# Linear attention of four images: from a loop of single stages to one staggered program

## The reference

```python
t = t + _L2_attn_ref(_ln_t(t), w_qkv, w_out, b_out)      # t: 4 x 1024 x 128, then _ln_t(t) feeds the mixtures

q, k, v = split(x @ w_qkv)                 # 8 heads of 32
k, v = inst_norm(k), inst_norm(v)          # (x - mean) / sqrt(var + 1e-5) over the 32 of a head
dots = einsum('bhnd,bhne->bhde', k, v)
out = einsum('bhnd,bhde->bhne', q, dots) * (1.0 / n)
return out.reshape(b, n, 256) @ w_out + b_out
```

## Time and profile before

| | |
|---|---|
| Median of 3 runs | 2886.87 us (2886.83 to 2897.33) |
| The profiled execution | 2889.75 us |
| Its span, first to last instruction | 2888.0 us |
| Mean granted TensorE clock | 0.781 of full speed |
| PE busy | 1869.1 us (65%) |
| DVE busy | 1648.0 us (57%) |
| ACT busy | 966.2 us (33%) |
| POOL busy | 658.1 us (23%) |

### The profile page before, as it was taken

How to read it: one execution, slowest core, us unless ns; L and a number is a source line. 1 busy time by engine, 2 the same in 40 slices (tenths; PEclk the granted TensorE clock), 3 DMA queues, 4 the chain that set the end, 5 groups by cost and what they waited for, 6 DMA issues and landing times. The chain is left out here.

```text
span 2888.0 us, 25863 instructions
## 1 busy us (share of the span) xinstructions
PE 1869.1 (65%) x8280; PEld 825.4 (29%) x8280; DVE 1648.0 (57%) x3684; ACT 966.2 (33%) x1542; POOL 658.1 (23%) x675
## 2 busy tenths in 40 slices
PE   1564893785686666599658888787886410190089
PEld 1121321321221334456312223232222210090034
DVE  3485776767768654466545756656562121088823
ACT  1232141142132131255326675665664210000133
POOL 2200600420330300044312132332123157500000
PEclk7686896787888776699859999998897655555589
DMA  3301201201200000020021110110000021100030
GB/s 86 80 18 28 59 2 43 58 0 39 50 15 18 7 0 0 0 86 18 14 66 35 27 56 14 30 42 25 24 5 9 5 63 10 8 8 31 2 124 22
DMA packets 58242, 88.62 MB, mean 31 GB/s; under 512 B 17992, under 2 KB 29250, under 8 KB 57866
## 3 DMA queue, kind: packets, MB, share of 16 engines
q1 hardware_dynamic: 47604, 77.66, 9.0%
q10 hardware_dynamic: 6426, 7.99, 1.3%
q0 software_dynamic: 4096, 1.58, 0.8%
HBM read 58.59 MB, written 24.74 MB: 29 GB/s over the span
## 5 line engine op out<-in xcount | busy, mean ns | idle before, releaser
L2150 DVE TENSOR_REDUCE f_half_max<-f_ring 128x1 f32<-128x512 f32 x512 | 334.8, 684 | 306.3 <-PE f_ring L1825 304.1
L2033 ACT ACTIVATE f_probs<-f_ST 128x512 f32<-128x512 f32 x512 | 293.0, 597 | 212.4 <-PE f_ST L1849 208.2
L1825 PE MATMUL f_ring<-f_stacks 96*128 96x512 bf16 x512 | 212.7, 417 | 54.4 <-DVE f_half_max L2150 27.6
L772 DVE TENSOR_REDUCE att_half_max<-att_ring 128x1 f32<-128x512 f32 x256 | 161.1, 683 | 101.4 <-PE att_ring L659 92.7
L1849 PE MATMUL f_ST<-f_stacks 99*128 99x512 bf16 x512 | 203.8, 404 | 11.6 <-ACT f_probs L2033 11.6
L2985 PE MATMUL ts_ps<-ts_tally 128*64 128x64 bf16 x1024 | 97.5, 357 | 167.4 <-issue 145.3
L755 ACT ACTIVATE att_probs<-att_ST 128x1024 f32<-128x1024 f32 x128 | 129.4, 1024 | 155.8 <-PE att_ST L684 155.6
L3020 DVE TENSOR_SCALAR ts_tally<-ts_digits 128x256 bf16<-128x256 bf16 x512 | 77.4, 231 | 166.4 <-PE ts_ps L2985 112.8
L1459 POOL TENSOR_TENSOR bm_h<-bm_h,bm_mix 128x512 f32<-128x512 f32 x64 | 82.2, 1305 | 316.6 <-DMA bm_mix<-mix 229.5
L1866 PE MATMUL f_O<-f_probs,f_v_ext 128*32 128x512 f32 x1024 | 153.0, 673 | 0.0
L2985 PEld LDWEIGHTS ts_ps<-ts_tally 128*64 128x64 bf16 x1024 | 91.9, 263 | 172.9 <-issue 150.8
(11 more groups left out here) (546 smaller groups left out, 3419.6 us busy)
## 6 DMA issues: line engine op xcount, KB each, us to landing
f_stacks<-f_parts SPq DMA_DIRECT2D x192, 64.0 KB, 2.2
gates_wide<-gates SPq DMA_DIRECT2D x16, 512.0 KB, 12.3
parts_dram<-l_parts SPq DMA_DIRECT2D x8, 768.0 KB, 4.1
stacks<-parts_dram SPq DMA_DIRECT2D x24, 256.0 KB, 9.4
stacks<-parts_dram ACTq DMA_DIRECT2D x24, 256.0 KB, 10.6
f_parts<-f_parts SPq DMA_DIRECT2D x8, 768.0 KB, 3.5
es_raw<-L_ffn_edge_index SPq DMA_DIRECT2D x8, 512.0 KB, 4.7
bm_mix<-mix SPq DMA_DIRECT2D x8, 512.0 KB, 9.6
```

Source lines behind the costliest of these rows:

```text
L772: nc.vector.tensor_reduce(half_max[:, h % 2, t, n:n + 1], ring[:, i % RING], AX.X, ALU.max, negate=True).then_inc(reduced, 1)
L1825: nc.tensor.matmul(ring[:, i % RING], f.stacks[0:STACK, 0, at, t * P:(t + 1) * P], f.stacks[0:STACK, 1, at, n * BANK:(n + 1) * BANK], star ...
L2033: nc.scalar.activation(f.probs[:, s % PROBS, n * BANK:(n + 1) * BANK], ST[:, i % HALVES], ACT.Exp).then_inc(probs_ready, 1)
L2150: nc.vector.tensor_reduce(f.half_max[:, h % 2, t, n:n + 1], ring[:, i % RING], AX.X, ALU.max, negate=True).then_inc(reduced, 1)
```

## The change

The loop of six stages is replaced by one stage for all images, `linear_attentions`. On each engine the four images' programs are interleaved by `Beside`, image b starting at turn 190 b; a program's turns run from 0 to 520, so up to three images are interleaved. The programs talk through counting semaphores that go on from image to image (a `Signal` counts to b x each + n; a `Bank` has one semaphore for filled and one for emptied).

- PSUM is split: two banks for transposes, two for kv, two for the output, one and a part for dots, mo and g. `xn` has a buffer for each of the two norms, `xc` and `kv` are doubled by image parity.
- The normalisation of the tiles goes from DVE to ACT (Identity with scale and bias per partition); DVE computes minus mean times inverse root in one instruction.
- Square comes before the copy on ACT. The sums of k and of v are turned to variances, multiplied with each other, and one root and one reciprocal of the product scale half of `kv` (256 columns), two tiles at a time.
- The bias is spread once to `f.bias` by one product and added to `t_tm` by POOL after the first norm; the one-row products are gone.
- mo is evacuated by one ACT copy of 256 columns.

Core of the diff (the declarations of buffers and semaphores, and most of the removed body, which is printed above, are left out):

```diff
-def linear_attention(nc, k, b):
...
-        layer_norm(nc, k, t_tm, xn[:], ps=ps, turned=xc)
...
-                    nc.tensor.matmul(ps[:, t], chunk(xc, t, P), k.w_kv[:], start=True, stop=True).then_inc(kv_ready, 1)
...
-                nc.tensor.matmul(o_, chunk(xc, 4 * i + t, P), g[:], start=True, stop=False)
-                last = nc.tensor.matmul(o_, k.ones_row[:], k.rows[0:1, 0, :], start=False, stop=True)
...
+class Linear:
+    STAGGER = 190
+    TURNED = (80, 500)
+    def __init__(self, nc, c):
         def sb(name, shape):
             return c.enter_context(sbuf(nc, name, shape, F32))
 
-        G = 16
-        t_tm, xn, xc = k.t_tm[:, b], sb("l2_xn", [P, NT, P]), sb("l2_xc", [P, N])
-        kv, sq = sb("l2_kv", [P, NT, 4 * P]), sb("l2_sq", [P, NT, 4 * P])
-        st = sb("l2_st", [P, NT, G])
-        dots, mo, g = sb("l2_dots", [P, 2, P]), sb("l2_mo", [P, 2, P]), sb("l2_g", [P, P])
-        ps = c.enter_context(psum(nc, "l2_ps", [P, 8, BANK], F32))
-        layer_norm(nc, k, t_tm, xn[:], ps=ps, turned=xc)
-        with stage(nc, "kv_ready", "copied", "squared", "chained", "rooted", "normed", "dots_ready", "masked") as (
-                block, kv_ready, copied, squared, chained, rooted, normed, dots_ready, masked):
-            def heads(x, t):
-                return x[:, t].rearrange("p (g d) -> p g d", d=32)
-
-            @block.tensor
-            def _(pe):
+        self.stats, self.s = sb("l2_stats", [P, 2, B, NT, 6]), sb("l2_s", [P, 2, B, NT, 3])
+        self.xn, self.xc = sb("l2_xn", [P, 2, NT, P]), sb("l2_xc", [P, 2, N])
+        self.kv, self.sq = sb("l2_kv", [P, 2, NT, 4 * P]), sb("l2_sq", [P, NT, 4 * P])
+        self.sums, self.scale = sb("l2_sums", [P, B, NT, 16]), sb("l2_scale", [P, B, NT, 8])
+        self.dots, self.mo, self.g, self.bias = (sb(f"l2_{n}", [P, w]) for n, w in (
+            ("dots", 2 * P), ("mo", 2 * P), ("g", P), ("bias", P)))
+        turns = sorted((b * self.STAGGER + at, w, b) for w, at in enumerate(self.TURNED) for b in range(B))
+        self.turned_use = {(w, b): i for i, (_, w, b) in enumerate(turns)}
+    def start(self, program):
+        return Beside(*((b * self.STAGGER, program(b)) for b in range(B)))
+def linear_attentions(nc, k):
...
+        @block.tensor
+        def _(pe):
+            nc.tensor.matmul(out_ps[:, 0, 0:P], k.ones_row[:], k.rows[0:1, 0, :], start=True, stop=True).then_inc(bias_ready, 1)
+            pe.wait_ge(bias_off, 1)
+            def transposes(w, b):
+                for u in range(2):
+                    yield f.TURNED[w] + 10 * u
+                    normed[w].wait(pe, b, u + 1)
+                    bank = turned[u].take(pe, f.turned_use[w, b])
+                    for t in range(4):
+                        last = nc.tensor.transpose(bank[:, t * P:(t + 1) * P], f.xn[:, w, 4 * u + t, :], k.ident[:])
+                    last.then_inc(turned[u].ready, 1)
+            def program(b):
+                xc, kv = f.xc[:, b % 2], f.kv[:, b % 2]
+                yield from transposes(0, b)
+                    yield 110 + 13 * t
+                    if t % 4 == 0:
+                        turned[t // 4].wait_off(pe, f.turned_use[0, b])
+                    i = NT * b + t
+                    if i >= 2:
+                        pe.wait_ge(kv_off, 2 * (i - 1))
+                    nc.tensor.matmul(kv_ps[:, i % 2], chunk(xc, t, P), k.w_kv[:], start=True, stop=True).then_inc(kv_ready, 1)
+                for q in range(4):
+                    yield 280 + 10 * q
+                    scaled.wait(pe, b, q + 1)
+                    if q == 0 and b >= 1:
+                        masked.wait(pe, b - 1)
+                        g_off.wait(pe, b - 1)
+                    for t in (2 * q, 2 * q + 1):
+                        for i in range(2):
+                            last = nc.tensor.matmul(dot_ps[:, i, 0:P], kv[:, t, (2 + i) * P:(3 + i) * P],
+                                                    kv[:, t, i * P:(i + 1) * P], start=(t == 0), stop=(t == NT - 1))
+                last.then_inc(dots_ready.sem, 1)
+                yield 330
+                masked.wait(pe, b)
+                for i in range(2):
+                    last = nc.tensor.matmul(dot_ps[:, 0, (1 + i) * P:(2 + i) * P], chunk(f.dots, i, P), k.w_o2[:, i],
+                                            start=True, stop=True)
+                last.then_inc(mo_ready.sem, 1)
+                yield 350
+                mo_off.wait(pe, b)
+                for j in range(2):
+                    last = nc.tensor.matmul(dot_ps[:, 0, 3 * P:4 * P], k.turned[:, k.t_q2 + j, :], chunk(f.mo, j, P),
+                                            start=(j == 0), stop=(j == 1))
+                last.then_inc(g_ready.sem, 1)
+                for u in range(2):
+                    yield 370 + 20 * u
+                    g_off.wait(pe, b)
+                    bank = outs[u].take(pe, b)
+                    for t in range(4):
+                        last = nc.tensor.matmul(bank[:, t * P:(t + 1) * P], chunk(xc, 4 * u + t, P), f.g[:], start=True,
+                                                stop=True)
+                    last.then_inc(outs[u].ready, 1)
+                yield from transposes(1, b)
+            f.start(program).finish()
+        @block.scalar
+        def _(act):
+            act.wait_ge(bias_ready, 1)
+            nc.scalar.copy(f.bias[:], out_ps[:, 0, 0:P]).then_inc(bias_off, 1)
+            def normalise(w, b, at):
+                s = f.s[:, w, b]
+                yield at
+                moments[w].wait(act, b)
+                nc.scalar.activation(s[:, :, 1], s[:, :, 1], ACT.Sqrt, bias=k.eps[:, 0:1]).then_inc(rooted[w].sem, 1)
+                for u in range(2):
+                    yield at + 20 + 10 * u
+                    scales[w].wait(act, b)
+                    if b >= 1:
+                        turned[u].wait(act, f.turned_use[w, b - 1])
+                    for t in range(4 * u, 4 * u + 4):
+                        last = nc.scalar.activation(f.xn[:, w, t, :], k.t_tm[:, b, t, :], ACT.Identity, bias=s[:, t, 2:3],
+                                                    scale=s[:, t, 1:2])
+                    last.then_inc(normed[w].sem, 1)
+            def program(b):
+                kv = f.kv[:, b % 2]
+                yield from normalise(0, b, 40)
+                yield 90
+                if b >= 2:
+                    outs[1].wait(act, b - 2)
+                bank = turned[0].wait(act, f.turned_use[0, b])
+                nc.scalar.copy(chunk(f.xc[:, b % 2], 0), bank).then_inc(turned[0].off, 1)
+                    yield 120 + 13 * t
+                    i = NT * b + t
+                    act.wait_ge(kv_ready, i + 1)
+                    if t == 0 and b >= 2:
+                        dots_ready.wait(act, b - 2)
+                    if b >= 1:
+                        summed.wait(act, b - 1, t + 1)
+                    nc.scalar.activation(f.sq[:, t], kv_ps[:, i % 2], ACT.Square).then_inc(kv_off, 1)
+                    nc.scalar.copy(kv[:, t], kv_ps[:, i % 2]).then_inc(kv_off, 1)
+                yield 250
+                multiplied.wait(act, b)
+                nc.scalar.activation(f.scale[:, b], f.scale[:, b], ACT.Sqrt).then_inc(kv_rooted.sem, 1)
+                yield 340
+                mo_ready.wait(act, b)
+                nc.scalar.copy(f.mo[:], dot_ps[:, 0, P:3 * P]).then_inc(mo_off.sem, 1)
+                yield 360
+                g_ready.wait(act, b)
+                if b >= 1:
+                    outs[1].wait(act, b - 1)
+                nc.scalar.copy(f.g[:], dot_ps[:, 0, 3 * P:4 * P]).then_inc(g_off.sem, 1)
+                yield from normalise(1, b, 460)
+                yield 510
+                bank = turned[0].wait(act, f.turned_use[1, b])
+                nc.scalar.copy(chunk(k.xn_cm[:, b], 0), bank).then_inc(turned[0].off, 1)
+            f.start(program).finish()
+        @block.vector
+        def _(dve):
+            chain = Chain(dve, chained)
+            def norm(w, b, at):
+                s, stats, x = f.s[:, w, b], f.stats[:, w, b], k.t_tm[:, b]
+                for u in range(2):
+                    yield at + 10 * u
+                    if w == 1:
+                        outs[u].wait_off(dve, b)
+                    for t in range(4 * u, 4 * u + 4):
+                        chain.add(nc.vector.bn_stats(stats[:, t, :], x[:, t, :]))
+                yield at + 20
+                chain.wait()
+                    last = nc.vector.bn_aggr(s[:, t, 0:2], stats[:, t, :])
+                last.then_inc(moments[w].sem, 1)
+                yield at + 50
+                rooted[w].wait(dve, b)
+                chain.link(nc.vector.reciprocal(s[:, :, 1], s[:, :, 1]))
+                nc.vector.scalar_tensor_tensor(s[:, :, 2], s[:, :, 0], -1.0, s[:, :, 1], ALU.mult,
+                                               ALU.mult).then_inc(scales[w].sem, 1)
+            def program(b):
+                kv = f.kv[:, b % 2]
```

(90 more changed lines are left out.)

43 lines of the change are left out of this document (removed).

## The result

The changed kernel takes 2817.44 us (median of 4 runs, 2813.07 to 2822.09), against 2886.85 us: a ratio of 0.9752, 95% interval 0.9733 to 0.9771. The forecast was 2815 us. The profiled execution took 2815.17 us, its span is 2813.4.

What follows compares the result with a forecast made beforehand. The stage was taken as a chain no engine fills: 193.9 us falls to 123.2 (16.5 + 21.5 + 59.2 + 26), saving 70.7 plus 0.9 at the exit, so 2815 us by the median; range 2805 to 2826.

Steps and rivals of the forecast that it cites:

- What bounds: Old image loop: a 193.9 us chain that no engine fills; what the stage loses the program loses, one for one.
- The sum: New stage: lead 16.5, second period 21.5, two full periods 59.2, tail 26, in all 123.2 us.
- Step (a): Start of a full period: DVE's additions, statistics, aggregations and three reduces before the moments of image b-1, 7.7 us.
- Step (b): ACT's root for b-1, eight normalisations of b, then the root for b-2 that DVE awaits: 3.8 us.
- Step (c): DVE's reciprocal, product and first scale before PE's dots can start: 1.1 us.
- Step (d): PE's line from dots to kv tile 6: 14.0 us, 2 for half clock, 1.0 for holes, 17.0 in all.
- Output products: PE's output matmuls: 11.7 us per image falls to 2.1 to 4.5 without one-row products; some 33 us saved in all.
- Edges and ACT's load: Five stage edges per image and the loop's end go, inside the 193.9 us; three ACT table loads count as nothing.
- Rival 1: Waits nearly vanish, DVE's 18 us plus 2 of waits bound the period: program 2791 us, chance 0.17.
- Rival 2: PE at half clock throughout the new stage: period 41.6 us, stage 164 us, program 2856 us, chance 0.18.
- Rival 3: Something serialises the images, no overlap: four times 41.5 us, stage 166 us, program 2858 us, chance 0.04.
- Rival 4: Fetching four straight-line copies of the loop body stalls the engines: slower, 2901 us or more, chance 0.02.

Runs made afterwards that it cites:

- e6: Changed kernel with the second norm's root first on ACT and GpSimd's bias addition after the masks: stage 112.3 us, program 2804.63 us, ratio 0.972.
- e2: Changed kernel with GpSimd's bias addition moved to wait for the masks instead of the first norm: stage 120.6 us, program 2817.07 us, ratio 0.974.
- e1: Changed kernel without GpSimd's bias addition, output bias left out: stage 120.6 us, program 2814.00 us, ratio 0.974.
- e9: As e7, with the spare products fitted to PE's idle stretches (6, 11, 11, 8 per image): stage 104.6 us, program 2795.26 us, ratio 0.967.
- e5: Kernel before the change without the one-row bias products, output bias left out: stage 162.3 us, program 2854.81 us, ratio 0.989.
- e4: Changed kernel with STAGGER 540 instead of 190, images one after another: stage 161.4 us, program 2854.95 us, ratio 0.987.
- e10: Changed kernel plus spare products nobody reads in PE's idle stretches, order and bias addition unchanged: stage 117.1 us, program 2807.11 us, ratio 0.972.
- e7: As e6, plus spare products nobody reads on PE, 3 at the start and 8 per image: stage 106.2 us, program 2799.65 us, ratio 0.969.

## Why the prediction was right

- *What bounds.* Right: the stage was a chain, its gain is the program's, one for one (71.7 and 1.0 at the exit, of 74.6; the other 1.9 are in code not touched).
- *The sum.* 123.2 against 122.2, and that it came so near is in part luck: three terms of the full period were mis-sized, one too low by 1.7 us and two too high by 0.8 and by 0.9 to 1.9, and they offset each other.
- *Step (a)*, 7.7 us: from 1047.58 to the product's end at 1054.45 are 6.9. The instructions are the ones forecast, three reduces and one addition among them; 0.25 us of the first statistics lies ahead of the cut, and the others follow each other more closely than their durations added up.
- *Step (b)*, 3.8: 1054.48 to 1058.29, 3.8. Right, and e6 against e2 shows that it was the order: 8.3 us of the stage for one turn.
- *Step (c)*, 1.1: 2.8 (1058.29 to 1061.09). The step that failed is the sentence that nothing waits for GpSimd's addition. Nobody waited for its result, but an instruction on the chain could not run beside it; a cover was named for the result and none for the port. It cost 1.7 us in each full period, and by e1 and e2 1.6 us in the stage.
- *Step (d)*, 17.0: 15.1 and 16.1 (1061.09 to 1076.22, 1089.74 to 1105.86). The start at half clock is there (0.63, 0.50). A rise at 1064.7, 3.6 us after the first dots, gives the 0.63 over 1061 to 1066; in the second full period it had not come 5.3 us after them. With the clock at 1.00 the same line takes 13.5 us in e9 (1055.93 to 1069.44), waits for banks included, where 14.0 and 1.0 for holes were forecast. So the half clock cost 1.6 and 2.6 us where 2 stood, and the products with their holes were put 1.5 too high.
- *Output products.* Priced at 3.3 us per image, the middle of the bounds; they run at 2.1, the low one, at a granted clock of 1.00. The one-row products were worth 31.6 us (e5) where 33 stood: 9.7 per image on the output products themselves, less what slower kv products (1.0) and dots (0.5) took back.
- *Edges and ACT's load.* They were never priced apart, since the new chain was summed from its pieces; e4 against e5 puts them at 0.9 us, together with the scales, the slower normalisation and the two-bank kv.
- *Rival 1* falls for this kernel: the root's place held the period off DVE's 18. With the root moved and the clock kept it comes to 22.9 (e9), with DVE at 16.4 us of work: still not DVE's. The sign named for this rival, a stage under 105 us, would not have told it apart: e9 has 104.6. *Rival 2* falls, 0.79 in the stage. *Rival 3*: that is e4, 161 us, and its price of 166 was near. *Rival 4* falls: no wait of microseconds for "issue" on the chain, and the lead of image 0, through cold code, took 16.3 us where 16.5 were summed from warm rows.
- *The chances.* The four that are faster by more than the threshold add up to 0.94, not 0.95, and 0.04 stood for within it, not 0.03.

## What to carry to other kernels

When programs are interleaved in a fixed order, list for each engine which wait stands ahead of which instruction of another image; a period is the sum of those, not the busiest engine, and one instruction of 0.3 us behind eight that need not precede it cost 3.4 us a period here (e2 against e6). Price a change of engine twice, by who waits for the result and by who cannot run meanwhile. And time saved just ahead of a PE at half clock can be lost again, as in e1, when the clock rises no sooner: remove the long wait, then feed PE through the short ones.

## What the runs showed of the hardware

- DVE's scalar_tensor_tensor of 8 columns with two SBUF tensors took 1.91 us beside GpSimd's tensor_tensor of 1024 columns, 0.17 without it, and a tensor_tensor of 512 columns 1.63 instead of 0.68 (e10); both ended after GpSimd's, the first 0.03 us and the second 0.56. Reduces (one tensor) beside it kept 0.68 us.
- While one-row products alternated with plain ones, TensorE's clock fell and stayed down though PE was hardly idle: in the earlier trace rows it stood at 0.54 through 11 us in which PE was busy 9.9, after 1.00. In the two full periods of e9, without one-row products and with PE busy 22.7 of 22.9 us, it was 1.00, and in e5 the plain output products took 0.13 us each, which is what L1416 takes at 1.00. That the single row is the reason is likely and not shown: no run changed the rows alone.
- The clock's fall did not follow the length of the wait alone: in e10 it fell among the products behind a wait of 3.9 us, while in the earlier trace rows it was still 1.00 at the end of four idle microseconds, and of two waits of 2.06 us in e7 one was followed by a fall and the other not.
